# Two token groups at a time: a new tile order in the state-to-model projection, with its weight blocks loaded once per pair of groups

## The chip, the cores and the metric

The program runs on all 8 cores of one Trainium2 chip. Each core takes 4096 of the 32768 tokens and works alone on them; all weights are given to every core. The metric is the device time of the slowest core in microseconds (us). The engines of a core have names of their own in the profile: PE is TensorE, DVE is VectorE, ACT is ScalarE, POOL is GpSimd, SP is SyncE. PEq, ACTq and SPq are the sequencers that issue instructions and DMAs.

## The reference

The function is one layer of two residual blocks on x of 16 x 2048 x 2048, float32:

```python
x = x + (tanh(layernorm(x) @ B.T) @ C.T + D * layernorm(x))      # B: 1024 x 2048, C: 2048 x 1024
h = layernorm(x)
x = x + (silu(h @ Wg.T) * (h @ Wu.T)) @ Wd.T                     # hidden size 5632
```

Wg, Wu and Wd are bytes with zero point 128 and one scale for each output row. Layernorm has no gain or bias, eps 1e-5.

## The kernel before

A preparation stage turns the bytes of the weights into bfloat16 images in device memory. Then come 8 passes; pass p takes 512 tokens as four groups g = 0 to 3 of 128 tokens. A pass has these stages, in TensorE's program order:

- State: 16 chains of 16 matmuls 128x256 (line 504) make B times the normalised tokens, kept feature-major in HFM1. ScalarE takes the tanh into SFM (line 328).
- AT, the projection back to 2048 features, which the change touches: 16 tiles (g, s), where s = 0 to 3 is a block of 512 output features. A tile is 4 small matmuls with the diagonal of D (line 517) and 8 matmuls 128x512 (line 526) with the two halves of a C block as moving operand. C blocks lie in four buffers WCB0 to WCB3 of 512 KB: s = 0 and 2 use WCB0 and WCB1, s = 1 and 3 use WCB2 and WCB3. VectorE adds each finished tile to the token buffer XT (line 453, here called the evacuation) and counts it in EV_AT. A tile's PSUM bank is one of four, so TensorE waits at tile m for the evacuation of tile m-4.
- Second normalisation, group by group, in an order written out by hand on two engines: ScalarE squares the group (line 334), VectorE makes mean and variance, ScalarE the root (line 337), VectorE applies it into HTM0 or HTM1 (line 428), ScalarE's queue issues a transposing DMA into HFM2 (line 342).
- Gate and up: the first gate work is cut in halves of tokens. Two chains of 16 matmuls 128x256 over groups 0 and 1 wait for the transposes of groups 0 and 1; two more over groups 2 and 3 wait for the transposes of groups 2 and 3 (line 536). Then come full chains of 128x512 (lines 536 and 546) for 44 hidden blocks, and the down projection (line 602).

Here the AT stage's tiles run s-pair first: tiles 0 to 7 are (g 0..3) x (s 0, 1), tiles 8 to 15 are (g 0..3) x (s 2, 3). So every C block is loaded once per pass. The second pair of blocks (line 208 on SP's queue) waits for the semaphore MM_AT, TensorE's count of finished tiles, at 7 for WCB0 and WCB1 and at 8 for WCB2 and WCB3. The first pair of the next pass is loaded ahead, during the gate stage's end. Group 0 is complete after tile 9, group 1 after tile 11, groups 2 and 3 after tiles 13 and 15 (tiles counted from 0), and VectorE runs a group's normalisation at those points of its order.

Of the kernel before, what the change touches and what calls it, by code (L numbers as in the profile page):

```python
# [20 lines left out]
G = 4  # L21
# [26 lines left out]
def build_nc(n_pass):  # L48
# [21 lines left out]
    with ExitStack() as ctx:  # L70
# [38 lines left out]
        sem = {}  # L109
# [23 lines left out]
        for _p in range(n_pass):  # L133
            for _s in range(SL):
                for _j in range(11):
# [3 lines left out]
                    _cnt_wd[key] = _cnt_wd.get(key, 0) + 16  # L139
                    wd_info[_u] = (special, _u % 3, _cnt_wd[key])  # L140

        AT_TILES = [(g, 2 * sp + si) for sp in range(2) for g in range(G)
                    for si in range(2)]
        AT_BANK = [2 * (s % 2) + (g % 2) for (g, s) in AT_TILES]

        ST_ORDER = []
# [16 lines left out]
        @block.sync  # L163
        def _(sync):
            for apsrc, sb in [(sgc, SGC), (suc, SUC),
                              (dcol, DCOL), (ident, IDENT)]:
                sync.dma_start(out=sb[:], in_=apsrc).then_inc(sem["LDC"], 16)

            def emit_prep_load(u):
                kind, i = unit_kind(u)  # L170
                if kind == "D" and i % 11 == 0:
                    s_ = i // 11
                    if s_ > 0:
                        sync.wait_ge(sem["P_DQ"], NU_B + NU_C + NU_G + NU_U + 11 * s_)
                    sync.dma_start(out=SDP[:], in_=sdq[s_]).then_inc(sem["LSDP"], 16)
                if kind in ("B", "C"):
                    if u >= 2:
                        sync.wait_ge(sem["P_DQ"], u - 1)
                    w = D if kind == "B" else NCH * 512
                    src = bmi[i] if kind == "B" else cmi[i]  # L180
                    sync.dma_start(out=BF32[u % 2][:, :w], in_=src).then_inc(PLD1[u % 2], 16)
                else:
                    o = u - (NU_B + NU_C)
                    if o >= 10:
                        sync.wait_ge(sem["P_DQ"], u - 10 + 1)
                    src = wgi[i] if kind == "G" else (wui[i] if kind == "U" else wdi[i])
                    sync.dma_start(out=LQ[o % 10][:], in_=src).then_inc(PLD2[o % 10], 16)

            for u in range(NUNITS):
                emit_prep_load(u)  # L190

            for i in range(8):
                sync.wait_ge(PWR[i], PWR_FINAL[i])

            def emit_b(p, half, n):
                u = 16 * p + 8 * half + n
                if u >= 3:
                    sync.wait_ge(sem["MM_ST"], u - 2)
                sync.dma_start(out=WBB[u % 3][:], in_=sb_img[n]).then_inc(LWB[u % 3], 16)

            def emit_c(p, sp, si, h2_):
                s = 2 * sp + si
                slot = 2 * si + h2_
                if p > 0 or sp > 0:
                    pm = (16 * p + 8 * (sp - 1) + 7 + si) if sp > 0 \
                        else (16 * (p - 1) + 15 + si)
                    sync.wait_ge(sem["MM_AT"], pm)
                sync.dma_start(out=WCB[slot][:],
                               in_=sc_img[s][:, h2_ * 4:(h2_ + 1) * 4, :]
                               ).then_inc(LWC[slot], 16)  # L210

            def emit_gu(p, hc, is_up):
                t = 2 * (HC * p + hc) + is_up
                if t >= 3:
                    hc3 = (t - 3) // 2
                    if (t - 3) % 2 == 0:
                        sync.wait_ge(sem["MM_G"], hc3 + 1)
                    else:
                        sync.wait_ge(sem["MM_U"], hc3 + 1)
                sync.dma_start(out=WGU[t % 3][:],  # L220
                               in_=(su_img if is_up else sg_img)[hc]
                               ).then_inc(LWGU[t % 3], 16)

            for p in range(n_pass):
                for half in range(2):
                    for n in range(NCH):
                        if p > 0 and half == 0 and n < 3:
                            continue
                        emit_b(p, half, n)
                for sp in range(2):  # L230
                    for si in range(2):
                        for h2_ in range(2):
                            if p > 0 and sp == 0:
                                continue
                            emit_c(p, sp, si, h2_)
                for hc in range(HC):
                    for is_up in range(2):
                        if p > 0 and 2 * hc + is_up < 3:
                            continue
                        emit_gu(p, hc, is_up)  # L240
                if p + 1 < n_pass:
                    for n in range(3):
                        emit_b(p + 1, 0, n)
                    for si in range(2):
                        for h2_ in range(2):
                            emit_c(p + 1, 0, si, h2_)
                for s in range(SL):
                    for j in range(11):
                        u = HC * p + 11 * s + j
                        if wd_info[u][0]:  # L250
                            continue
                        if u >= 3:
                            sync.wait_ge(sem["FR_D"], u - 2)
                        sync.dma_start(out=WDB[u % 3][:],
                                       in_=sd_img[s * 11 + j]).then_inc(LWD[u % 3], 16)
                if p + 1 < n_pass:
                    for q in range(3):
                        emit_gu(p + 1, q // 2, q % 2)
            for b in range(NXB):
                n_st = len([1 for gi in range(4 * n_pass) if gi % NXB == b])  # L260
                if n_st:
                    sync.wait_ge(STX[b], 16 * n_st)
# [32 lines left out]
        def _(scalar):  # L295
# [27 lines left out]
            for p in range(n_pass):  # L323
# [5 lines left out]
                                      AF.Tanh).then_inc(sem["TANH"], 1)  # L329
                for g in range(G):  # L330
                    k = 8 * p + 4 + g
                    scalar.wait_ge(sem["EV_AT"], 16 * p + 2 * g + 10)
                    scalar.wait_ge(TPS[(k - 2) % 4], 16 * ((k - 2) // 4 + 1))
                    scalar.activation(HTM[k % 2][:], XT[xb(p, g)][:], AF.Square,  # L334
                                      accum_out=S2T[:, 4 + g:5 + g]).then_inc(sem["SQ_A"], 1)
                    scalar.wait_ge(sem["FIN"], k + 1)
                    scalar.activation(STDT[:, 4 + g:5 + g], VART[:, 4 + g:5 + g],
                                      AF.Sqrt).then_inc(sem["SQRT_A"], 1)
                    scalar.wait_ge(sem["APPLY"], k + 1)
                    if p > 0:  # L340
                        scalar.wait_ge(sem["MM_U"], HC * p)
                    scalar.dma_start(out=HFM2[:, :, g * 128:(g + 1) * 128],
                                     in_=HTM[k % 2][:], transpose=True).then_inc(TPS[k % 4], 16)
# [23 lines left out]
        def _(vector):  # L367
# [81 lines left out]
            for p in range(n_pass):  # L449
                def at_evac(m):  # L450
                    g, s = AT_TILES[m]
                    vector.wait_ge(sem["MM_AT"], 16 * p + m + 1)
# [2 lines left out]
                        1.0, XT[xb(p, g)][:, s * 512:(s + 1) * 512], ALU.mult, ALU.add,  # L455
                        accum_out=S1PT[:, g, s:s + 1]).then_inc(sem["EV_AT"], 1)

                for m in range(8):
                    at_evac(m)
                for g in range(G):  # L460
                    at_evac(8 + 2 * g)
                    at_evac(8 + 2 * g + 1)
                    k = 8 * p + 4 + g
                    vector.wait_ge(sem["EV_AT"], 16 * p + 2 * g + 10)
                    htm_free(k)
                    ds_inc(vector.tensor_scalar(TR4[:], S1PT[:, g, :], 1.0, 0.0, ALU.mult,
                                                ALU.add, accum_out=S1T[:, 4 + g:5 + g]))
                    ln_finalize(k, 4 + g, sqa=4 * p + g + 1)
                    ln_apply(k, 4 + g, xb(p, g))
# [19 lines left out]
        def _(tensor):  # L489
            tensor.wait_ge(sem["DDIAG_OK"], 1)  # L490
            for p in range(n_pass):
# [16 lines left out]
                for m in range(16):  # L508
                    g, s = AT_TILES[m]
# [5 lines left out]
                    for sub in range(4):  # L515
# [3 lines left out]
                                      DDIAG[:, dcg, :],  # L519
                                      start=(sub == 0), stop=False)  # L520
                    ins = None
                    for n in range(NCH):
                        if n % 4 == 0:
                            tensor.wait_ge(LWC[2 * (s % 2) + n // 4],
                                           16 * (2 * p + s // 2 + 1))
                        ins = tensor.matmul(PS[:, bank, :],  # L526
                                            SFM[:, n, g * 128:(g + 1) * 128],
                                            WCB[2 * (s % 2) + n // 4][:, n % 4, :],
                                            start=False, stop=(n == NCH - 1))
# [126 lines left out]
```

## Time and profile before

| | us |
|---|---|
| median of 3 runs | 5090.84 (5089.77 to 5103.79) |
| profiled execution | 5099.44 |
| its span, slowest core | 5097.9 |
| spans of the 8 cores | 5066.3 to 5097.9 |
| TensorE matmul busy | 4257.4 (84%) |
| granted TensorE clock, mean | 0.963 to 0.968 |

The span goes from the first instruction to the last on the slowest core, core 2, whose trace is read here. The profiled execution is 8.6 us above the median of the runs, and the time outside the span is 1.5 us. The preparation takes until about 465 us; after that one pass takes about 580 us. The eight AT stages begin at 510.5, 1085.3, 1667.3, 2256.7, 2834.5, 3416.5, 3991.8 and 4571.9 us.

### The profile page before, as it was taken

The numbers are of one execution on the slowest core, as the hardware profiler recorded it, in microseconds if no ns is written. First come the engines' busy times: TensorE is split into PE (matmuls) and PEld (weight loads), VectorE is DVE, ScalarE is ACT, GpSimd is POOL, SyncE is SP. The second block draws the span as 40 slices with busy tenths as digits, with TensorE's granted clock in tenths as the row PEclk, the third lists the DMA queues.
The fourth block names the chain that finished last, engine by engine and source line by source line (L and its number), as shares of the span: only waits on it lengthen the run. The fifth ranks groups of instructions, "written<-read, shape, count | busy, mean of one in ns | idle before, by whom it ended". The sixth has DMA issues, their size and how long they took to land.

```text
span 5097.9 us, 52159 instructions; the slowest of 8 cores (5066.3 to 5097.9 us)
## 1 busy us (share of the span) xinstructions
PE 4257.4 (84%) x20736; PEld 2048.7 (40%) x20736; DVE 936.7 (18%) x1408; ACT 397.7 (8%) x576; POOL 94.4 (2%) x179
## 2 busy tenths in 40 slices
PE   0002899979998899978999799988999799988998
PEld 0002444444444444444444444444444444444444
DVE  3465212021121111111120111211120211211100
ACT  0000100010100111001000101001100110001100
POOL 1210000000000000000000000000000000000000
PEclk9999999989999999989999899999999899999999
DMA  9987445554456445554455544554454544554544
GB/s 310 323 298 240 157 153 177 157 168 163 153 178 198 133 153 169 161 157 157 153 178 177 153 152 150 182 182 149 153 178 167 161 152 152 181 180 130 153 149 161
DMA packets 364905, 891.67 MB, mean 175 GB/s; under 512 B 159360, under 2 KB 159360, under 8 KB 353920
## 3 DMA queue, kind: packets, MB, share of 16 engines
q1 hardware_dynamic: 197136, 693.81, 41.7%
q10 hardware_dynamic: 142336, 100.68, 7.6%
q0 software_dynamic: 25200, 93.86, 5.5%
q8 instruction: 173, 2.83, 0.2%
q14 instruction: 60, 0.49, 0.0%
HBM read 743.53 MB, written 111.15 MB: 168 GB/s over the span
## 4 chain that ended last, share of the span: by engine, by line
PE 74%; DMA 17%; DVE 4%; ACT 2%; issue 1%; SPq 1%; ACTq 1%; DVEq 0%; POOLq 0%
PE PS L602 24%; PE PS L536 23%; PE PS L546 23%; PE PS L526 3%; DMA LQ<-wgi 2%; PE PS L504 2%; DMA WDB<-sd_img 2%; DMA LQ<-wui 2%; DMA WBB<-sb_img 2%; DMA HFM<-HTM 2%; DMA LQ<-wdi 1%; ACT HTM L334 1%; DMA XT<-xin 1%; DMA WCB<-sc_img 1%; DMA out<-XT 1%
## 5 line engine op out<-in xcount | busy, mean ns | idle before, releaser
L536 PE MATMUL PS<-HFM,WGU 128*128 128x512 bf16 (+1 forms) x5888 | 1308.1, 378 | 118.2 <-DMA HFM<-HTM 116.4
L546 PE MATMUL PS<-HFM,WGU 128*128 128x512 bf16 x5632 | 1280.5, 381 | 21.9 <-DMA WGU<-su_img 21.9
L602 PE MATMUL PS<-WDB,GFM 128*128 128x512 bf16 x5632 | 1233.5, 382 | 44.8 <-DMA WDB<-sd_img 44.8
L536 PEld LDWEIGHTS PS<-HFM,WGU 128*128 128x128 bf16 x5888 | 591.5, 101 | 781.9 <-issue 124.8
L602 PEld LDWEIGHTS PS<-WDB,GFM 128*128 128x128 bf16 x5632 | 554.9, 99 | 723.2 <-issue 69.8
L546 PEld LDWEIGHTS PS<-HFM,WGU 128*128 128x128 bf16 x5632 | 552.5, 98 | 692.1 <-issue 35.4
L504 PE MATMUL PS<-HFM,WBB 128*128 128x256 bf16 x2048 | 278.2, 303 | 609.2 <-DMA HFM<-HTM 526.7
L473 DVE SCALAR_TENSOR_TENSOR GFM<-PS,SUC,GFM 128x512 bf16<-128x512 f32 x352 | 264.6, 752 | 2233.3 <-PE PS L546 2233.3
L504 PEld LDWEIGHTS PS<-HFM,WBB 128*128 128x128 bf16 x2048 | 218.3, 108 | 669.1 <-issue 622.0
L351 ACT ACTIVATE GFM<-PS,SGC 128x512 bf16<-128x512 f32 x352 | 241.7, 687 | 2152.8 <-PE PS L536 2152.7
L526 PE MATMUL PS<-WCB,SFM 128*128 128x512 bf16 x1024 | 256.1, 394 | 24.6 <-DMA WCB<-sc_img 24.5
L481 DVE TENSOR_TENSOR XT<-XT,PS 128x512 f32<-128x512 f32 x128 | 79.4, 683 | 1045.9 <-PE PS L602 1045.9
L453 DVE SCALAR_TENSOR_TENSOR XT<-PS,XT 128x512 f32<-128x512 f32 x128 | 86.5, 689 | 400.7 <-PE PS L526 400.7
L526 PEld LDWEIGHTS PS<-WCB,SFM 128*128 128x128 bf16 x1024 | 96.7, 100 | 126.0 <-issue 42.6
L380 DVE TENSOR_SCALAR WOUT<-LQ 128x2048 bf16<-128x2048 uint8 x88 | 107.9, 1229 | 110.2 <-DMA LQ<-wui 56.6
L386 DVE SCALAR_TENSOR_TENSOR WOUT<-LQ,SDP 128x2048 bf16<-128x2048 uint8 x44 | 97.4, 2286 | 33.7 <-DMA LQ<-wdi 33.7
L312 ACT ACTIVATE STDT<-VART 128x1 f32<-128x1 f32 x32 | 6.5, 203 | 1243.4 <-DVE VART L416 1243.3
L291 POOL DMA_DIRECT2D WDB<-sd_img x31 | 16.7, 538 | 4599.8 <-PE PS L602 4599.8
L437 DVE TENSOR_SCALAR_CACHE_REDUCE HTM<-XT 128x2048 bf16<-128x2048 f32 x32 | 73.0, 2280 | 102.5 <-DMA XT<-xin 102.5
L428 DVE TENSOR_SCALAR HTM<-XT,MEANT,RSTDT 128x2048 bf16<-128x2048 f32 x64 | 86.2, 1346 | 6.9
L334 ACT ACTIVATE HTM<-XT 128x2048 bf16<-128x2048 f32 x32 | 61.1, 1910 | 296.1 <-DVE XT L453 292.0
L441 DVE SCALAR_TENSOR_TENSOR HTM<-XT 128x2048 bf16<-128x2048 f32 x32 | 73.4, 2293 | 3.4
(29 smaller groups left out, 349.6 us busy)
## 6 DMA issues: line engine op xcount, KB each, us to landing
WGU<-sg_img SPq DMA_DIRECT2D x352, 512.0 KB, 3.5
WGU<-su_img SPq DMA_DIRECT2D x352, 512.0 KB, 3.5
WDB<-sd_img SPq DMA_DIRECT2D x321, 512.0 KB, 3.5
WBB<-sb_img SPq DMA_DIRECT2D x128, 512.0 KB, 5.7
XT<-xin ACTq DMA_DIRECT2D x32, 1024.0 KB, 8.3
WCB<-sc_img SPq DMA_DIRECT2D x64, 512.0 KB, 6.9
out<-XT ACTq DMA_DIRECT2D x32, 1024.0 KB, 8.8
sg_img<-WOUT POOLq DMA_DIRECT2D x44, 512.0 KB, 14.2
```

Of the source, the lines that this page charges most:

```text
L334: scalar.activation(HTM[k % 2][:], XT[xb(p, g)][:], AF.Square, accum_out=S2T[:, 4 + g:5 + g]).then_inc(sem["SQ_A"], 1)
L351: scalar.activation(GFM[:, hc, :], PS[:, 4 + hc % 2, :], AF.Silu, scale=SGC[:, hc:hc + 1]).then_inc(sem["SILU"], 1)
L380: vector.tensor_scalar_add(WOUT[u % 8][:, :D], LQ[o % 10][:], -128.0).then_inc(sem["P_DQ"], 1)
L386: vector.scalar_tensor_tensor(WOUT[u % 8][:, :D], LQ[o % 10][:], -128.0, SDP[:], ALU.add, ALU.mult).then_inc(sem["P_DQ"], 1)
L428: vector.tensor_scalar(HTM[k % 2][:], XT[b][:], MEANT[:, i:i + 1], RSTDT[:, i:i + 1], ALU.subtract, ALU.mult).then_inc(sem["APPLY"], 1)
L453: vector.scalar_tensor_tensor(XT[xb(p, g)][:, s * 512:(s + 1) * 512], PS[:, AT_BANK[m], :], 1.0, XT[xb(p, g)][:, s * 512:(s + 1) * 512], A ...
L473: vector.scalar_tensor_tensor(GFM[:, hc, :], PS[:, 6 + hc % 2, :], SUC[:, hc:hc + 1], GFM[:, hc, :], ALU.mult, ALU.mult).then_inc(sem["GMU ...
L504: ins = tensor.matmul(PS[:, n, lo:hi], WBB[u % 3][:, c, :], HFM1[:, c, lo:hi], start=(c == 0), stop=(c == DC - 1))
L526: ins = tensor.matmul(PS[:, bank, :], SFM[:, n, g * 128:(g + 1) * 128], WCB[2 * (s % 2) + n // 4][:, n % 4, :], start=False, stop=(n == NC ...
L536: ins = tensor.matmul(PS[:, 4 + hc % 2, lo:hi], WGU[t % 3][:, c, :], HFM2[:, c, lo:hi], start=(c == 0), stop=(c == DC - 1))
L546: ins = tensor.matmul(PS[:, 6 + hc % 2, lo:hi], WGU[t % 3][:, c, :], HFM2[:, c, lo:hi], start=(c == 0), stop=(c == DC - 1))
L602: ins = tensor.matmul(PS[:, bank, :], GFM[:, hc, g * 128:(g + 1) * 128], WDB[u % 3][:, q * 512:(q + 1) * 512], start=(hc == 0), stop=(hc = ...
```

## The change

The 16 tiles run in another order: group pair first. Tiles 0 to 3 are (g 0, 1) x (s 0, 1), tiles 4 to 7 are (g 0, 1) x (s 2, 3), tiles 8 to 11 are (g 2, 3) x (s 0, 1), tiles 12 to 15 are (g 2, 3) x (s 2, 3). Groups 0, 1, 2 and 3 are complete after tiles 5, 7, 13 and 15. The C blocks are loaded in four blocks `blk` of four DMAs per pass in place of two, and the waits and counts follow.

```diff
-        AT_TILES = [(g, 2 * sp + si) for sp in range(2) for g in range(G)
-                    for si in range(2)]
+        AT_TILES = [(2 * gp + gi, 2 * sp + si) for gp in range(2) for sp in range(2)
+                    for gi in range(2) for si in range(2)]
...
-            def emit_c(p, sp, si, h2_):
-                s = 2 * sp + si
+            def emit_c(p, blk, si, h2_):
+                s = 2 * (blk % 2) + si
                 slot = 2 * si + h2_
-                if p > 0 or sp > 0:
-                    pm = (16 * p + 8 * (sp - 1) + 7 + si) if sp > 0 \
+                if p > 0 or blk > 0:
+                    pm = (16 * p + 4 * blk - 1 + si) if blk > 0 \
                         else (16 * (p - 1) + 15 + si)
                     sync.wait_ge(sem["MM_AT"], pm)
...
-                for sp in range(2):
+                for blk in range(4):
                     for si in range(2):
                         for h2_ in range(2):
-                            if p > 0 and sp == 0:
+                            if p > 0 and blk == 0:
                                 continue
-                            emit_c(p, sp, si, h2_)
+                            emit_c(p, blk, si, h2_)
...
-                    scalar.wait_ge(sem["EV_AT"], 16 * p + 2 * g + 10)
+                    scalar.wait_ge(sem["EV_AT"], 16 * p + (6, 8, 14, 16)[g])
...
-                for m in range(8):
-                    at_evac(m)
+                AT_LAST = (5, 7, 13, 15)
+                _m = 0
                 for g in range(G):
-                    at_evac(8 + 2 * g)
-                    at_evac(8 + 2 * g + 1)
+                    while _m <= AT_LAST[g]:
+                        at_evac(_m)
+                        _m += 1
                     k = 8 * p + 4 + g
-                    vector.wait_ge(sem["EV_AT"], 16 * p + 2 * g + 10)
+                    vector.wait_ge(sem["EV_AT"], 16 * p + AT_LAST[g] + 1)
...
+                    blk = 2 * (g // 2) + s // 2
                     for n in range(NCH):
                         if n % 4 == 0:
                             tensor.wait_ge(LWC[2 * (s % 2) + n // 4],
-                                           16 * (2 * p + s // 2 + 1))
+                                           16 * (4 * p + blk + 1))
```

On VectorE, at the AT stage of pass 0 (XT0 to XT3 are the four groups' token buffers; rows of line 453 evacuate a tile, the row of line 466 or 467 begins a group's normalisation):

```order
 L453 SCALAR_TENSOR_TENSOR XT0,S1PT<-PS,XT0 128x512 x2
 L453 SCALAR_TENSOR_TENSOR XT1,S1PT<-PS,XT1 128x512 x2
-L453 SCALAR_TENSOR_TENSOR XT2,S1PT<-PS,XT2 128x512 x2
-L453 SCALAR_TENSOR_TENSOR XT3,S1PT<-PS,XT3 128x512 x2
-L453 SCALAR_TENSOR_TENSOR XT0,S1PT<-PS,XT0 128x512 x2
-L466 TENSOR_SCALAR TR4,S1T<-S1PT 128x4
+L453 SCALAR_TENSOR_TENSOR XT0,S1PT<-PS,XT0 128x512 x2
+L467 TENSOR_SCALAR TR4,S1T<-S1PT 128x4
```

Group 0's normalisation stands after 6 evacuations in place of 10.

On VectorE, further on in the same stage, between the normalisations of group 1 and group 2:

```order
 L428 TENSOR_SCALAR HTM1<-XT1,MEANT,RSTDT 128x2048
 L453 SCALAR_TENSOR_TENSOR XT2,S1PT<-PS,XT2 128x512 x2
-L466 TENSOR_SCALAR TR4,S1T<-S1PT 128x4
+L453 SCALAR_TENSOR_TENSOR XT3,S1PT<-PS,XT3 128x512 x2
+L453 SCALAR_TENSOR_TENSOR XT2,S1PT<-PS,XT2 128x512 x2
+L467 TENSOR_SCALAR TR4,S1T<-S1PT 128x4
```

Six evacuations stand between these two normalisations in place of two; groups 2 and 3 keep their places, after 14 and 16 evacuations.

On SP's queue, at the end of the C block loads of pass 0:

```order
 L208 DMA WCB2<-sc_img 128x2048 [waits MM_AT]
 L208 DMA WCB3<-sc_img 128x2048 [waits MM_AT]
+L208 DMA WCB0<-sc_img 128x2048 [waits MM_AT]
+L208 DMA WCB1<-sc_img 128x2048 [waits MM_AT]
+L208 DMA WCB2<-sc_img 128x2048 [waits MM_AT]
+L208 DMA WCB3<-sc_img 128x2048 [waits MM_AT]
```

The same four rows follow once more: 8 DMAs of 512 KB are added in every pass, ahead of the gate stage's loads. ScalarE's order is the same as before. TensorE's has the same shapes in a row, with other groups and C blocks behind them.

## Rows read from the trace of the kernel before

**Rows 1.** The page: busy time by engine, and the WCB load's issues.
```profile
PE 4257.4 (84%) x20736; PEld 2048.7 (40%) x20736; DVE 936.7 (18%) x1408; ACT 397.7 (8%) x576; POOL 94.4 (2%) x179
...
WCB<-sc_img SPq DMA_DIRECT2D x64, 512.0 KB, 6.9
```

**Rows 2.** Waits of TensorE (who <- for whom: us in total, times, longest us).
```profile
PE PS L536 <- DMA HFM<-HTM: 116.4, 16, 8.2
...
PE PS L526 <- DMA WCB<-sc_img: 24.5, 18, 3.3
```

**Rows 3.** Timeline of pass 1, TensorE: start, duration, what, [idle before <-releaser].
```profile
1085.25 0.38 PE L517 MATMUL PS<-DDIAG,HFM 128*128 128x128 bf16 x4 [0.95 <-ACT SFM L328]
...
1104.02 1.02 PE L526 MATMUL PS<-WCB,SFM 128*128 128x512 bf16 x4 [2.79 <-DMA WCB<-sc_img]
...
1105.27 1.87 PE L526 MATMUL PS<-WCB,SFM 128*128 128x512 bf16 x4 [0.22 <-DMA WCB<-sc_img]
...
1107.35 2.41 PE L526 MATMUL PS<-WCB,SFM 128*128 128x512 bf16 x8
...
1119.85 1.89 PE L526 MATMUL PS<-WCB,SFM 128*128 128x512 bf16 x8
...
1128.73 5.37 PE L536 MATMUL PS<-HFM,WGU 128*128 128x256 bf16 x32 [6.99 <-DMA HFM<-HTM]
...
1142.07 5.53 PE L536 MATMUL PS<-HFM,WGU 128*128 128x256 bf16 x32 [7.97 <-DMA HFM<-HTM]
```

**Rows 4.** The same timeline of pass 1: VectorE, ScalarE and the two DMA queues.
```profile
1087.47 0.69 DVE L453 SCALAR_TENSOR_TENSOR XT<-PS,XT 128x512 f32<-128x512 f32 x1 [31.05 <-PE PS L526]
...
1099.14 2.75 SPq L208 DMA_DIRECT2D WCB<-sc_img  x4
...
1099.17 0.69 DVE L453 SCALAR_TENSOR_TENSOR XT<-PS,XT 128x512 f32<-128x512 f32 x1 [1.25 <-PE PS L526]
...
1109.87 0.69 DVE L453 SCALAR_TENSOR_TENSOR XT<-PS,XT 128x512 f32<-128x512 f32 x1 [1.93 <-PE PS L526]
...
1110.71 1.91 ACT L334 ACTIVATE HTM<-XT 128x2048 bf16<-128x2048 f32 x1 [25.72 <-DVE XT L453]
...
1117.06 1.85 ACTq L342 DMA_TRANSPOSE HFM<-HTM  x1
...
1124.13 1.78 ACTq L342 DMA_TRANSPOSE HFM<-HTM  x1
...
1126.06 1.91 ACT L334 ACTIVATE HTM<-XT 128x2048 bf16<-128x2048 f32 x1 [3.78 <-DVE XT L453]
...
1137.68 1.92 ACTq L342 DMA_TRANSPOSE HFM<-HTM  x1
```

**Rows 5.** Timelines of passes 2 and 4: first matmul, and tile 9's evacuation.
```profile
1667.25 0.38 PE L517 MATMUL PS<-DDIAG,HFM 128*128 128x128 bf16 x4 [0.95 <-ACT SFM L328]
...
1691.18 0.69 DVE L453 SCALAR_TENSOR_TENSOR XT<-PS,XT 128x512 f32<-128x512 f32 x1 [1.58 <-PE PS L526]
...
2834.54 0.38 PE L517 MATMUL PS<-DDIAG,HFM 128*128 128x128 bf16 x4 [0.95 <-ACT SFM L328]
...
2860.30 0.69 DVE L453 SCALAR_TENSOR_TENSOR XT<-PS,XT 128x512 f32<-128x512 f32 x1 [2.51 <-PE PS L526]
```

**Rows 6.** Stretches of pass 1: busy us of each engine, PEclk, DMA share, GB/s.
```profile
1116.90:1121.90 5.00, 4.72 (x28) 2.04 (x25) 1.86 (x10) 2.00 (x2) 0.00 (x0) 1.00 0.56 105
...
1099.10:1108.80 9.70, 6.69 (x33) 2.98 (x31) 2.10 (x6) 0.00 (x0) 0.00 (x0) 0.82 0.67 216
1099.10:1104.00 4.90, 2.14 (x16) 1.03 (x14) 1.40 (x4) 0.00 (x0) 0.00 (x0) 1.00 0.74 186
1104.00:1108.80 4.80, 4.56 (x17) 1.95 (x18) 0.70 (x2) 0.00 (x0) 0.00 (x0) 0.64 0.61 247
```

**Rows 7.** Line 317, the first normalisation's transposes, which run beside WBB loads.
```profile
L317 ACTq DMA_TRANSPOSE HFM<-HTM x32: 1334/2151/4104, 452.9 to 4542.7; - x32
...
DMA to landing us min/median/max: 4.3/6.1/15.6
```

## The prediction

> **What bounds the kernel now.** I read the page first: TensorE's matmuls are busy for 84% of the span and no other engine comes near it [rows 1], so time is won or lost only where TensorE stands still. TensorE's list of waits comes next, and two of its rows belong to the edited stage [rows 2]: the gate stage's wait for the transposes into HFM2, 116.4 us in 16 waits, so two of 7.3 us in each of the 8 passes, and the AT stage's wait for C blocks, 24.5 us in all, so 3.1 us a pass. The change trades one for the other. To price the trade I follow one pass, pass 1, in the timeline, on TensorE [rows 3] and on the engines around it [rows 4]. All times below count from the first matmul of its AT stage, 1085.25.
>
> The first evacuation starts at 2.22 (1087.47). The seventh starts at 1099.17, 11.70 later for 6 tiles: a tile takes 1.95 us. Then the C blocks are exchanged. Call this a refill. Its four loads are issued from 1099.14 on, when tile 6 is done, so only tile 7 covers them: WCB0 is there at 1104.02 and WCB1 at 1105.27, 4.9 and 6.1 us after the issue. The evacuation of tile 9 starts at 1109.87, which is 24.62. Without the refill it would be 2.22 + 9 x 1.95 = 19.77, so a refill costs 4.85 us, more than the 2.79 + 0.22 us of idle time beside it. The rest is the clock: the granted clock is 1.00 in the 4.9 us from the issue and 0.64 in the next 4.8 [rows 6], after TensorE stood idle for 2.79; four matmuls take 1.87 us there and the next eight 2.41 [rows 3]. In passes 2 and 4 tile 9's evacuation starts at 23.93 and 25.76 [rows 5], so the refill costs 4.16 and 5.99. The mean of the three is 5.0.
>
> From tile 9 on, nothing of TensorE sets the end. Squaring of group 0 starts 0.84 after the evacuation (1110.71), and the four groups follow each other through ScalarE, VectorE and the issue of the transpose, until the last transpose is issued at 1137.68 and the second half of the gate work starts at 1142.07, which is 56.82. TensorE has been ready since 1119.85 + 1.89 and fills the time with only one piece of 5.37 us, at 1128.73.
>
> **The change part by part.** *What it removes.* Groups 0 and 1 complete before tile 8, so their normalisation lies beside tiles 6 to 12, and their 13.4 us of chain (transposes issued 1117.06 and 1124.13, the second 13.4 after the first squaring) leave the path. What is late next is group 2, complete only after tile 13, and group 3 behind it. Their part can be read off: squaring of group 2 at 1126.06 to the gate work at 1142.07 is 16.01 us. With the 0.84 before it, 16.85 us from the evacuation of tile 13. The half chains over groups 0 and 1 start at once after tile 15 and are over long before; they cost nothing. Group 3's tiles 14 and 15 are done 2 x 1.95 us after tile 13, inside group 2's chain, as it is today.
>
> *What it adds.* Each pass has three refills in place of one, because each C block is used by two groups before its buffer is taken for another. The loads of each refill are again issued one tile before they are needed (MM_AT 3, 7, 11 for WCB0 and WCB1, needed by tiles 4, 8, 12). 64 more loads of 512 KB in all. Behind the waiting loads on SP's queue stand only the gate stage's loads, and in passes 1 to 7 the first three of those are already there, so nobody else waits.
>
> The sum, with refill 1 at pass 1's own 4.85 and the two new ones at 5.0: tile 13's evacuation starts at 2.22 + 13 x 1.95 + 4.85 + 10.0 = 42.42, the gate work's second half at 42.42 + 16.85 = 59.27, against 56.82. That is 2.45 us a pass later, 19.6 us in 8 passes. The break-even is a new refill at 3.8 us. With both at 4.16 the sum is +0.8 a pass (+6 us), with both at 5.99 it is +4.4 (+35 us).
>
> *A collision that the trace of before does not have.* Refills 2 and 3 now meet transposes. A transpose takes 0.56 x 5.0 = 2.8 us of all the DMA engines, a refill 0.67 x 9.7 = 6.5 us, of which 0.74 x 4.9 = 3.6 lie in the first 4.9 us after the issue [rows 6]; so it works from 1.3 to 7.8 us after its issue. Group 0's squaring starts 0.84 after tile 5's evacuation (2.22 + 9.75 + 4.85 = 16.8), its transpose is issued 7.2 us after that evacuation as today (1109.87 to 1117.06), at 24.0, and works until 28. Refill 2 is issued with tile 6 done, at 18.8, and works from 20.1 to 26.6: an overlap of some 1.3 us. Group 1's transpose is issued 7.1 later, at 31.1, and works from 32.4 to 35.2; refill 3, issued at 31.6, works from 32.9 to 39.4: an overlap of 2.3, and its first block is the one that TensorE stands waiting for. The lower end is 0, if the loads go first or the clock's share of the refill hides the delay; a gain is excluded, as more traffic brings no load sooner. The near upper end is the whole of both overlaps, 3.6 us a pass. The nearest rows on mixed traffic are the transposes of the first normalisation, which run beside WBB loads and stores: 6.1 us to landing in the median, 15.6 at most, 4.3 at best [rows 7]. I take half of 3.6, that is 1.8 a pass or 14 us, since the rows show each kind filling the engines and none going first.
>
> The Trainium skill ("DMA: Bandwidth & Descriptors", section "Issuing engines are not separate DMA queues") says that DMAs of ScalarE's and SP's queues end up on the same 16 DMA engines and interleave. By that rule a load and a transpose both lose; without it the sum would stop at +20. No run here shows a C load beside a transpose yet.
>
> *Edits that cost nothing.* TensorE's wait for the evacuation of tile m-4: VectorE is in group 0's normalisation from 16.8 to 24.0 and in group 1's until 31.1, with evacuations 6 and 7 between. Tile 12 needs evacuation 8, done by 32, and its C block does not come before 36. Were this cover gone, each microsecond of refill 3 saved would be lost here again from about 4 us on. ScalarE's order is unchanged.
>
> **Sum.** 19.6 + 14 = 34 us. The profiled execution is 5099.44, with 1.5 us outside its span, and would become about 5134; it lies 8.6 above the median of the runs, 5090.84, and I put the difference on that median: 5125.
>
> **The rivals.**
>
> A, the forecast: new refills near 5 us, partly stretched. 5110 to 5146 (+20 to +35 by the refills' spread, 0 to 29 for the overlaps, not both at their ends). 0.50.
>
> B, no collision, new refills at 5.0: +20, 5111. For it: two thirds of each refill lie outside the transposes. Against it: refill 3 does not. 0.14.
>
> C, heavy collision: the small packets of the transposes hold the loads back for more than their own work. Landings of 15.6 us [rows 7] speak for it; against it, those also lie beside 1 MB stores. If the overlapped 3.6 us are stretched as the slowest of those transposes is, 15.6 / 4.3 = 3.6 times, they become 13, which is 9.4 us later a pass, 75 in 8, on top of 20: 5186. From 5147 on I count it here. 0.16.
>
> D, the new refills are all as cheap as the cheapest seen, 4.16, and the transposes hide: +6, 5097. 0.13.
>
> E, the other side: a new refill costs only its first idle gap. If TensorE's clock stays at 2.4 GHz, its higher level, through the new refills, because each is followed and preceded by dense tiles, and the second and third buffers arrive under running tiles, each costs 2.8 us in place of 5.0. Then the gate work starts at 2.22 + 25.35 + 4.85 + 5.6 + 16.85 = 54.87, 1.95 sooner than now: -16 us, 5075. It decides from below 3.8 us a refill. Against it: all three refills read above cost over 4.1, and the clock fell to 0.64 after one idle gap of 2.8. 0.07.
>
> **How the numbers follow.** A measurement of this kernel tells about 0.3%, or 15 us, from no change: slower is above 5106, faster below 5076. A, B and C are slower: 0.80. D and a part of E are within: 0.15. The rest of E is faster: 0.05. The time is A's, 5125. The range 5097 to 5160 holds A, B, a part of D and the near part of C; the likeliest case alone is 5110 to 5146.
>
> **What would show it.** Waits of TensorE: the C block row near 24.5 x 3, with some 50 waits, where C loads before had 18; the transposes' row falls from 116.4 to about 76 (one wait a pass, 16.85 less 3.9 for tiles 14 and 15 and 3.5 for the first half chains at full clock, 9.5), since the first half chains wait for nothing. Timeline of a pass: tile 13's evacuation 42 to 45 after the AT stage's start, the second half of the gate work at 59 to 63, and the half chains over groups 0 and 1 directly behind tile 15. Granted clock below 1 after each of the three refills. A median landing of C loads above 6.9 [rows 1]. I am wrong if tile 13's evacuation starts before 40, or if the distance from it to the gate work is not about 17, or if TensorE waits for VectorE at tile 12.

## The result and the profile after

The changed kernel is slower: the ratio to the kernel before is 1.0121, with a 95% interval of 1.0097 to 1.0145, so 49 to 74 us. (Many of the runs, of both kernels, had one die at a lower granted clock; they set the medians over all runs, 5189.23 and 5170.76 us, while the ratios here leave them out, and "not determined" stands where too few others are left.) The profiled execution took 5153.61 us, its slowest core 5152.1, against 5099.44 and 5097.9 before. The forecast was +34 us, with slower at 0.80. On the median of before, 5090.84, the ratio makes 5152 us: above the likeliest case (5110 to 5146) and in the stretch that the prediction gave to rival C (from 5147 on).

The page after, for [rows 1]:

```profile
PE 4264.8 (83%) x20736; PEld 2046.6 (40%) x20736; DVE 935.4 (18%) x1408; ACT 397.6 (8%) x576; POOL 96.9 (2%) x179
...
WCB<-sc_img SPq DMA_DIRECT2D x128, 512.0 KB, 6.8
```

TensorE's waits after, for [rows 2] (us in total, times, longest):

```profile
PE PS L528 <- DMA WCB<-sc_img: 127.4, 61, 15.9
...
PE PS L538 <- DMA HFM<-HTM: 72.6, 8, 9.8
...
PE PS L548 <- DMA WGU<-su_img: 13.6, 7, 2.8
PE PS L518 <- DVE XT L453: 2.5, 3, 1.0
```

The transposes' waits fall from 116.4 to 72.6 us, one a pass, as forecast (76). The waits for C blocks rise from 24.5 to 127.4 where 73 was forecast (24.5 x 3), in 61 waits where 50 were, and the longest is 15.9 us. Pass 1 of the changed kernel shows where, for [rows 3] and [rows 4]; times in the text count from its AT start, 1109.50:

```profile
1109.50 0.38 PE L518 MATMUL PS<-DDIAG,HFM 128*128 128x128 bf16 x4 [0.95 <-ACT SFM L328]
...
1122.74 0.69 DVE L453 SCALAR_TENSOR_TENSOR XT<-PS,XT 128x512 f32<-128x512 f32 x1 [4.47 <-PE PS L528]
...
1131.83 1.02 PE L528 MATMUL PS<-WCB,SFM 128*128 128x512 bf16 x4 [2.04 <-DMA WCB<-sc_img]
...
1132.96 4.20 ACTq L342 DMA_TRANSPOSE HFM<-HTM  x1
...
1142.73 5.82 ACTq L342 DMA_TRANSPOSE HFM<-HTM  x1
...
1148.94 1.02 PE L528 MATMUL PS<-WCB,SFM 128*128 128x512 bf16 x4 [0.17 <-DMA WCB<-sc_img]
...
1156.82 1.87 PE L528 MATMUL PS<-WCB,SFM 128*128 128x512 bf16 x4 [6.85 <-DMA WCB<-sc_img]
...
1158.80 0.69 DVE L453 SCALAR_TENSOR_TENSOR XT<-PS,XT 128x512 f32<-128x512 f32 x1 [9.55 <-PE PS L528]
1158.91 3.52 PE L528 MATMUL PS<-WCB,SFM 128*128 128x512 bf16 x8
...
1164.21 3.66 PE L538 MATMUL PS<-HFM,WGU 128*128 128x256 bf16 x32
...
1171.26 1.93 ACTq L342 DMA_TRANSPOSE HFM<-HTM  x1
...
1175.65 0.59 PE L538 MATMUL PS<-HFM,WGU 128*128 128x256 bf16 x2 [7.78 <-DMA HFM<-HTM]
```

Refills 1 and 2 go as forecast: tile 5 is evacuated from 16.3 (1125.77; 16.8 forecast) and refill 2 holds TensorE for 2.04 us at tile 8. Refill 3 does not. Its last block arrives at 1156.82, in the middle of tile 13, after 6.85 us of waiting. Tile 13's evacuation starts at 49.3 (1158.80), where the sum had 42.4 to 46. From there to the second half of the gate work it is 16.85 us, exactly as forecast. The half chains over groups 0 and 1 (1164.21) follow tile 15 directly and take 3.66 us in place of 5.37.

ScalarE's queue shows the other party. Issuing group 0's transpose takes 4.20 us where it took 1.85 [rows 4], so group 1 follows late: its transpose is issued at 33.2, not 31.1. Refill 3's first two loads were issued at 31.0, when tile 10 was done, and its second two at 33.0 to 33.4, so the transpose leaves with the second two. Issuing it takes 5.82 us. Landing of the second normalisation's 32 transposes (line 342):

```profile
DMA to landing us min/median/max: 4.2/4.9/22.1
```

Landing of the 128 C loads (line 208):

```profile
DMA to landing us min/median/max: 4.0/6.8/21.6
```

One transpose took 22.1 and one C load 21.6 us, while the medians, 4.9 and 6.8, hardly moved (4.3 and 6.9 before): the damage sits in a few transfers. Over all cores and passes it is group 1's transpose that lands late, 13.8 us after its issue on average (4.3 before); groups 2 and 3 land after 4.3 as before, group 0 after 6.0. The stretches of refill 3 in pass 1, with the columns of [rows 6]:

```profile
1142.70:1156.80 14.10, 5.18 (x20) 1.89 (x21) 3.04 (x10) 0.00 (x0) 0.00 (x0) 0.71 1.11 166
...
1145.00:1148.00 3.00, 2.81 (x8) 0.84 (x7) 0.04 (x2) 0.00 (x0) 0.00 (x0) 0.52 1.19 238
...
1154.00:1157.00 3.00, 0.18 (x1) 0.14 (x2) 0.00 (x0) 0.00 (x0) 0.00 (x0) 0.50 1.07 72
```

All DMA engines stay busy (a share above 1 means that packets' times overlap in the records), but what they move falls from 238 to 72 GB/s. Their busy time in this stretch, the time of all packets over 16 engines, is 1.11 x 14.1 = 15.7 us. I call it engine time; where the share is above 1 it can hold waiting as well as work. A refill alone was 6.5 and a transpose alone 2.8 [rows 6].

**The same over all cores.** From every core's timeline I took the time from the first matmul of the AT stage to the start of the second half of the gate work, here "the stretch". Each value is the mean of 8 cores x 8 passes. The ratio is to the kernel before.

| kernel | stretch, us | AT stage alone, us | ratio (95%) |
|---|---|---|---|
| before | 57.16 | 36.56 | 1 |
| changed | 65.03 | 52.60 | 1.0121 (1.0097 to 1.0145) |
| hold_transposes | 58.90 | 45.40 | 1.0058 (1.0036 to 1.0081) |
| hold_group1_only | 59.67 | 46.13 | not determined |
| plain_copy | 60.15 | 46.58 | 1.0062 (1.0036 to 1.0087) |
| timed_plain | 61.91 | 48.38 | 1.0101 (1.0077 to 1.0126) |
| kept_old_order | 52.49 | 31.88 | 0.9832 (0.9809 to 0.9854) |
| kept_new_order | 49.80 | 36.63 | 0.9798 (0.9763 to 0.9832) |
| kept_late_group1 | 45.24 | 31.91 | 0.9712 (0.9692 to 0.9732) |
| kept_group_major | 42.91 | 32.18 | 0.9682 (0.9648 to 0.9716) |
| kept_group_major_fill | other stage | 32.04 | 0.9689 (0.9665 to 0.9713) |
| group_major_fill_late_x | other stage | 32.21 | 0.9581 (0.9532 to 0.9629) |

The last six kernels of the table keep C blocks on chip. In the last two the first gate work is cut at another token, so the stretch would end at another piece of work ("other stage"). The change costs 7.87 us a pass in the stretch, 63 us in 8. From the stretch's end to the next AT stage the mean goes from 522.41 to 520.70, 12 us back in 7 passes. Together 51 us; the profiled spans differ by 54, the ratio says 61.

### The profile page after: what moved, and what is told of

Same layout as the page of the kernel before. It is cut to its first block, busy times and chain, and to the rows that moved or that the text cites. A ratio compares the mean times of both kernels' runs of the same rounds, so it can differ in the third digit from the quotient of the medians.

```text
span 5152.1 us, 52287 instructions; the slowest of 8 cores (5121.6 to 5152.1 us)
## 1 busy us (share of the span) xinstructions
PE 4264.8 (83%) x20736; PEld 2046.6 (40%) x20736; DVE 935.4 (18%) x1408; ACT 397.6 (8%) x576; POOL 96.9 (2%) x179
## 4 chain that ended last, share of the span: by engine, by line
PE 74%; DMA 19%; DVE 3%; issue 1%; SPq 1%; ACT 1%; ACTq 0%; DVEq 0%; POOLq 0%
PE PS L604 23%; PE PS L538 23%; PE PS L548 22%; DMA WCB<-sc_img 4%; PE PS L528 3%; PE PS L505 2%; DMA WDB<-sd_img 2%; DMA WBB<-sb_img 2%; DMA HFM<-HTM 2%; DMA su_img<-WOUT 1%; DMA sg_img<-WOUT 1%; DMA XT<-xin 1%; DMA out<-XT 1%; DMA LQ<-wdi 1%; DMA LQ<-wgi 1%
## 5 line engine op out<-in xcount | busy, mean ns | idle before, releaser
L538 PE MATMUL PS<-HFM,WGU 128*128 128x512 bf16 (+1 forms) x5888 | 1289.9, 374 | 73.1 <-DMA HFM<-HTM 72.6
L528 PE MATMUL PS<-WCB,SFM 128*128 128x512 bf16 x1024 | 287.8, 425 | 127.6 <-DMA WCB<-sc_img 127.4
```

The costliest lines, as they stand in the source:

```text
L528: ins = tensor.matmul(PS[:, bank, :], SFM[:, n, g * 128:(g + 1) * 128], WCB[2 * (s % 2) + n // 4][:, n % 4, :], start=False, stop=(n == NC ...
L538: ins = tensor.matmul(PS[:, 4 + hc % 2, lo:hi], WGU[t % 3][:, c, :], HFM2[:, c, lo:hi], start=(c == 0), stop=(c == DC - 1))
```

## The experiments

My theory after the result: refill 3 and group 1's transpose meet on the DMA engines, and together they take more engine time than one after the other. The rival: refills are simply dearer than 5 us when there are three of them, through device memory or the clock.

**Hold both transposes.** Before the transposes of groups 0 and 1 ScalarE waits for the refill in flight:

```diff
+                    if g in (0, 1):
+                        for i in range(4):
+                            scalar.wait_ge(LWC[i], 16 * (4 * p + 3 + g))
                     scalar.dma_start(out=HFM2[...], in_=HTM[k % 2][:], transpose=True)
```

> The changed kernel, but ScalarE's queue issues the transposes of groups 0 and 1 only when the refill in flight (refill 2, refill 3) has landed. From AT start to the second half of the gate work, mean over 8 cores and 8 passes: 57.16 us before, 65.03 changed. Theory 'collision': the transposes hold refill 3 back; with them out of the way the stretch is 59.2 to 60, as the sum without a collision had it, the time falls by 5 to 6 us a pass, about 43 us, ratio to before about 1.004, and the waits for C blocks fall from 127 us to about 75. Rival 'refills are dearer by themselves' (device memory or clock): no change, 65 us and ratio 1.012.

The stretch was 58.90 us: 6.1 of the 7.87 us are gone, by nothing but a later issue, with the three refills still there. The rival is out as the cause of these 6.1 us. TensorE's waits on core 0, this profile's slowest:

```profile
PE PS L541 <- DMA HFM<-HTM: 78.8, 11, 10.1
...
PE PS L531 <- DMA WCB<-sc_img: 56.7, 53, 4.7
...
PE PS L521 <- DVE XT L456: 20.9, 8, 3.9
```

The C blocks' row fell below the forecast (about 75), to 56.7, but VectorE's rose to 20.9: the held transpose of group 0 pushes group 1's normalisation back, and tile 12 waits for evacuation 8, beside the refill it would wait for anyway. In pass 1 of core 2 refill 3 and the transpose stand apart:

```profile
1116.30:1124.70 8.40, 3.38 (x15) 1.48 (x14) 4.48 (x13) 2.21 (x3) 0.00 (x0) 0.83 0.85 298
1124.70:1129.70 5.00, 4.78 (x19) 2.14 (x19) 0.70 (x2) 0.00 (x0) 0.00 (x0) 0.60 0.56 105
```

That is 0.85 x 8.4 = 7.1 and 0.56 x 5.0 = 2.8 us of engine time, 9.9 in all, against 15.7 when they met. (The first stretch also holds the end of group 0's held transpose.) Counted over all cores and passes 1 to 7, from the first issue of refill 3 and group 1's transpose to the last landing of the two, for 2.6 MB each time, it is 14.1 us in the changed kernel and 9.4 with group 1's transpose held (the next run).

**Hold group 1's only** (`if g in (1,)`).

> The changed kernel with only group 1's transpose held until refill 3 has landed; group 0's is issued beside refill 2 as in the changed kernel. Holding both gave 58.90 us from the AT start to the second half of the gate work, the changed kernel 65.03. If all of the loss lies in refill 3 and group 1's transpose: 59 to 60, ratio as with both held, about 1.006. Rival, group 0's transpose costs its share too (it may still be in flight when refill 3 starts): 61 to 62.5, ratio about 1.009.

59.67 us. Group 1's transpose in refill 3 makes 5.4 of the 6.1 us, group 0's the other 0.8. The first reading holds. TensorE's wait for C blocks is 70.4 us here, close to the 73 forecast for three refills without a collision, and its wait for VectorE only 4.0.

**A plain copy in place of the transposes**, in passes 1 to 7:

```diff
+                    if p > 0 and g < 2:
+                        scalar.dma_start(out=GFM[:, 8 + 4 * g:12 + 4 * g, :],
+                                         in_=HTM[k % 2][:]).then_inc(TPS[k % 4], 16)
+                        continue
```

> The changed kernel; in passes 1 to 7 the transposing DMAs of groups 0 and 1 are replaced by plain DMAs of the same 512 KB, between the same engines and at the same place, into an unused part of GFM (so HFM2 keeps the groups 0 and 1 of pass 0; the output is not the reference's). If it is the kind of the transfer, its 2080 small packets, that holds refill 3 back: near 60 us for the stretch, ratio about 1.004. If any 512 KB beside a refill would do it: between 61 and 65, ratio 1.007 to 1.012. If refills are dearer by themselves: 65 and 1.012.

60.15 us, which looks like "the kind of transfer". But the moment changed too: a plain copy is issued in 0.5 us, so group 1's left on average 0.7 us ahead of refill 3's first load, where the changed kernel's transpose leaves 1.6 us behind it. This run cannot tell kind from timing.

**The same moment, two kinds.** Group 0's copy is plain in both, and group 1's transfer waits for tile 10, so it leaves with refill 3, once as a plain copy and once as a transpose:

```diff
+                    if p > 0 and g == 1:
+                        scalar.wait_ge(sem["MM_AT"], 16 * p + 11)
```

> The changed kernel; in passes 1 to 7 group 0's transpose is a plain DMA of 512 KB into an unused part of GFM, and so is group 1's, which is issued only when tile 10 is done (MM_AT 11), in the moment in which refill 3 is issued (the output is not the reference's). With plain_copy group 1's copy left before refill 3, so that it could not tell kind from timing. If the kind of transfer makes the loss: the stretch stays near 60 us, at most 61.5, and the engines' work in refill 3 is about 6.5 + 1.7 us. If any transfer of 512 KB in this moment does it: 63 or more.

> The same kernel with one difference: group 1's transfer is the transposing DMA again, issued in the same moment (MM_AT 11); group 0's stays a plain copy (the output is not the reference's). Theory 'kind': 64 to 66 us as in the changed kernel, 4 to 5 more than timed_plain, and the engines' work in refill 3 above 12 us. Rival 'two transposes in a row are needed' (group 0's still in flight): 61 or less. Rival 'any transfer': the same as timed_plain.

Over passes 1 to 7 the stretch is 61.70 us (standard error 0.27) with the plain copy and 65.05 (0.44) with the transpose; but cores 4 to 7 had a granted clock of 0.90 in the transpose's profile. On cores 0 to 3 alone, with 0.963 to 0.966 and 0.958 to 0.963, it is 61.65 and 64.23. The transpose's ratio is not determined. Over the same passes the copies that left early give 59.75, holding group 1's transpose 59.28, and holding both 58.55. The truth lies between my two theories: 512 KB of any kind in this moment cost 2 to 3 us a pass (61.70 less 59.75, 59.28 or 58.55), and that it is a transpose another 2.6. The stretches after the issue on core 2, pass 1, with the plain copy:

```profile
1114.40:1119.40 5.00, 2.05 (x13) 0.92 (x11) 2.33 (x8) 0.00 (x0) 0.00 (x0) 1.00 0.91 256
1119.40:1124.40 5.00, 4.47 (x18) 1.70 (x17) 0.70 (x2) 0.00 (x0) 0.00 (x0) 0.66 0.66 269
1124.40:1127.40 3.00, 3.00 (x22) 1.59 (x21) 0.86 (x4) 1.73 (x1) 0.00 (x0) 1.00 0.00 0
```

And with the transpose:

```profile
1116.60:1121.60 5.00, 2.06 (x14) 0.92 (x11) 2.30 (x8) 0.00 (x0) 0.00 (x0) 1.00 0.94 226
1121.60:1126.60 5.00, 2.62 (x10) 0.94 (x8) 0.70 (x2) 0.00 (x0) 0.00 (x0) 0.57 1.08 194
1126.60:1131.60 5.00, 4.06 (x13) 1.73 (x14) 0.38 (x1) 0.00 (x0) 0.00 (x0) 0.50 0.59 104
```

7.9 us of engine time with the plain copy, 13.1 with the transpose, for the same bytes; over all cores and passes 1 to 7, counted as above, 7.9 and 13.0. The rival that needs two transposes in a row is out: here group 0's is a plain copy.

**No refills.** The tanh output moves into an unused part of GFM, six C half blocks stay on chip for the whole kernel, and only the two of s = 3 are loaded once a pass:

```diff
-        SFM = E(nc.sbuf_tensor("SFM", [128, NCH, T], BF16))
+        SFM = GFM
-        WCB = [... for i in range(4)]
+        WCB = [... for i in range(6)]
...
+                dst = WCB[2 * s + h2_][:] if s < 3 else \
+                    GFM[:, 24 + 4 * h2_:28 + 4 * h2_, :]
```

> The tile order of before with the same kept C blocks and no refill: it prices the refill of before alone. My price of 4.9 us a refill gives 52.3 for the stretch, -39 us, ratio 0.992. If only the idle gap counts (3.3 us): -26 us, 0.995. The difference to the new order with kept blocks is what the new order is worth by itself: about 63 us.

> The changed kernel's tile order without refills: SFM lies in a part of GFM, six C half blocks (s = 0 to 2) stay on chip for the whole kernel, and the two of s = 3 are loaded once a pass into an unused part of GFM around the AT stage's start. Both theories: no refill left, tile 13's evacuation at 27.6 and the second half of the gate work at 44.4 after the AT start, 12.7 a pass earlier than before, 102 us in all, ratio about 0.980. If the normalisation chain of groups 0 and 1 on VectorE then stops TensorE (tile 12 waits for evacuation 8), some 2 to 4 us a pass less of it, ratio 0.983 to 0.986.

With the old order the stretch was 52.49 us, as priced (52.3), so a refill is worth 4.7 us and not only its idle gap. The ratio 0.9832 is 85 us, twice the forecast. The other half has another place:

```profile
PE PS L530 <- DMA HFM<-HTM: 117.4, 16, 8.4
...
PE PS L596 <- DMA WDB<-sd_img: 3.2, 2, 2.8
```

The down stage's wait for its first D blocks fell from 44.8 us before to 3.2. Before, four C loads for the next pass stood ahead of these D loads on SP's queue; now they are gone. I had counted the removed loads at nothing. That they are what held the D loads back is likely but not shown, as no run took out these four alone; the same row fell from 42.0 us in the changed kernel to 5.6 with the new order and kept blocks.

With the new order the stretch was 49.80, not 44.4. The second reading of the expectation came true, and larger:

```profile
PE PS L511 <- DVE XT L446: 26.0, 9, 3.5
```

On core 2, pass 1, the last matmuls of tile 11 and the first of tile 12:

```profile
1086.35 1.89 PE L521 MATMUL PS<-WCB,GFM 128*128 128x512 bf16 x8
1091.62 0.38 PE L511 MATMUL PS<-DDIAG,HFM 128*128 128x128 bf16 x4 [3.37 <-DVE XT L446]
```

VectorE is in group 1's normalisation when tile 12 needs evacuation 8: 3.37 us of standing, and a granted clock of 0.66 in the 5 us behind it. So the new tile order as written is worth 2.7 us a pass even with no refill at all. It needs one more edit:

```diff
-                AT_LAST = (5, 7, 13, 15)
+                AT_LAST = (5, 9, 13, 15)
```

> The new tile order with kept C blocks, and VectorE takes evacuations 8 and 9 ahead of group 1's normalisation (AT_LAST of group 1 is 9). Kept blocks alone gave 49.80 us where the sum without stalls has 44.4, and TensorE waited for VectorE at tile 12 (3.37 us in pass 1, then half clock). If that wait is the whole missing part: 44.5 to 46 us, 4 to 5 us a pass, ratio about 0.973. Rival, the chain of groups 2 and 3 itself is longer than read: 49 us stays, 0.980.

45.24 us and 0.9712: the wait was 4.6 of the 5.4 us that were missing, and VectorE's row is back to 0.4 us.

**A version that beats both.** With all C blocks on chip the tiles can go group by group, banks `m % 4`:

```diff
+        AT_TILES = [(g, s) for g in range(G) for s in range(SL)]
+        AT_BANK = [m % 4 for m in range(16)]
```

> Kept C blocks and tiles group by group, (g, s) with s inside, banks m % 4; each group is complete 4 tiles after the one before. VectorE's cycle for a group (7.2 us of chain and 4 evacuations, about 7.7) then just fits TensorE's 4 tiles (7.8). Sum: squarings at 8.9, 18, 25.8 and 33.6, second half of the gate work at 43.1 after the AT start against 49.8: 6.7 a pass, 54 us, ratio about 0.969. If each group's chain stops TensorE as in the new order (3 us a group and half clock): 50 or more, ratio 0.98 or above.

42.91 us (43.1 forecast), ratio 0.9682. What is left is one wait of some 7 us for group 3's transpose. The next edit fills it by cutting the first gate and up chains at token 384:

```diff
-                    gate_chain(hc, 0, 256, False)
+                    gate_chain(hc, 0, 384, False)
+                up_chain(0, 0, 384, False)
...
-                    gate_chain(hc, 256, 512, True)
+                    gate_chain(hc, 384, 512, True)
+                up_chain(0, 384, 512, True)
```

> The same, and the first gate and up work is cut at token 384 in place of 256: three chains over groups 0 to 2 (gate 0, gate 1, up 0) fill the wait for group 3's transpose, then three of 128 tokens over group 3. Sum: the three long chains take 7.7 us from 35.3 on, the short ones 3 us from 43.1, where now 3.4 to 5.5 of half chains and 3.4 of up 0 follow: 4 to 6 us a pass less, 32 to 48 us, ratio about 0.961. If the short chains of 128 columns are dearer than their columns, nothing is gained: 0.969.

The time stayed (0.9689), and not for the reason that the second reading gives. The chains came where they should, but nothing was won, because the next wait took the gain:

```profile
1103.67 5.36 PE L531 MATMUL PS<-HFM,WGU 128*128 128x384 bf16 x32 [3.62 <-DMA HFM<-HTM]
...
1113.25 1.06 PE L541 MATMUL PS<-HFM,WGU 128*128 128x128 bf16 x16
1123.31 4.52 PE L541 MATMUL PS<-HFM,WGU 128*128 128x512 bf16 x15 [9.00 <-DMA WGU<-su_img]
```

Up 1 waits 9.00 us for its weights, which are loaded beside 3 MB of tokens; this row went from 10.7 us in all to 51.5. Moving those token loads behind gate blocks 8, 12 and 16:

```diff
+                    if hc in (8, 12, 16) and p + 1 < n_pass:
+                        emit_xload(p + 1, hc // 4 - 2)
```

> Kept C blocks, tiles group by group, and the three loads of the next pass's tokens are issued from ScalarE's queue ahead of gate blocks 8, 12 and 16 instead of directly behind the last transpose. The wait for WGU<-su_img at the stage's start is 10.7 us in 7 waits with group-major tiles; moved loads should take most of it: 8 us less, ratio 0.967 against 0.968. If those waits have nothing to do with the token loads: no change.

> The cut at token 384 with the token loads moved in the same way. With the cut alone the time stayed (0.9689 against 0.9682) and TensorE waited 51.5 us in 8 waits for WGU<-su_img, which is loaded beside 3 MB of tokens. If the token loads cause it: the load lands about 3.5 us after its issue, the wait shrinks from 9 to about 3 us, 5 to 6 us in 7 passes, 35 to 40 us, ratio about 0.961. If the wait is that WGU0 comes free too late, only 1 to 2 us a pass are won: 0.966.

The ratio of the first of the two is not determined; on its core 4 the row for WGU<-su_img has 0.3 us left of 10.7, but the row for the D blocks has 14.9 where it had 5.1, so whether time was won stays open. The second reached 0.9581 (0.9532 to 0.9629), 4879.79 us in its profiled execution. TensorE's waits there:

```profile
PE PS L530 <- DMA HFM<-HTM: 27.4, 8, 3.6
PE PS L540 <- DMA WGU<-su_img: 22.6, 12, 4.1
```

## Why the prediction was wrong

The direction and the trade were right, the size was not: +34 forecast, 49 to 74 measured. The step that failed is the price of the collision of refills 2 and 3 with the transposes: 1.8 us a pass forecast, 6.1 measured, of which 5.4 lie in refill 3 and group 1's transpose.

- *Two waits of 7.3 us become one.* Right: 72.6 us in 8 waits, 76 forecast.
- *A refill costs 5.0 us.* Right, within 0.3. Tile 5's evacuation at 16.3 against 16.8; the old order without its refill came out 4.7 us shorter; and with group 1's transpose held, three refills cost 59.67 less 45.24, so 4.8 each.
- *Tail of 16.85 us behind tile 13's evacuation.* Right to the hundredth in pass 1.
- *The sum without a collision, 59.27 us.* It matches the runs in which the transposes were held (58.90, 59.67). The match is partly luck with both held, since a wait for VectorE stood in for part of refill 3 there.
- *The collision, "half of 3.6, that is 1.8 a pass".* This is the step that failed. Measured it is 65.03 less 58.90, so 6.1 us a pass. Two things were wrong in it. First, and small, the time of meeting: I let group 1's transpose leave at 31.1, half a us ahead of refill 3, but the stretched issue of group 0's (4.20 us) delayed it to 33.2, two us behind refill 3's first load. By my own working times that raises the overlap only from 2.3 us to the transpose's whole 2.8. Second, and decisive, I took the engines' work as conserved: 6.5 + 2.8 = 9.3 us, in whatever order. It was 15.7 in pass 1, and 14.1 on average against 9.4 apart. My upper end, the whole of both overlaps, rested on the same assumption and was no bound. Rival C had the right mechanism ("hold the loads back for more than their own work"), and I gave it 0.16 and a price of 9.4 us; the truth lies between A and C. Not all of it is the small packets of a transpose: the plain copy in the same moment cost 2 to 3 us too.
- *TensorE does not wait for VectorE at tile 12.* Wrong as written, and I had named it a sign of being wrong: it waits there in 3 of core 2's passes (2.5 us in all), and in 37 of 64 over all cores, up to 1.3 us. It costs next to nothing, for the reason given: refill 3, which tile 12 needs anyway, comes later still. The runs with kept blocks took that cover away, and the same wait was worth 4.6 us of stretch (49.80 less 45.24).
- *The other signs.* The half chains came directly behind tile 15, as forecast. Tile 13's evacuation (49.3) and the second half of the gate work (66.2 in pass 1) came later than the 42 to 45 and 59 to 63 named. The median landing of C loads did not rise above 6.9 (it is 6.8), and in pass 1 the granted clock fell behind refills 1 and 3 (0.66 and 0.50 over 5 us) but not behind refill 2 (1.00).
- *The Trainium skill's rule* that DMAs of the two queues interleave on the same 16 engines ("DMA: Bandwidth & Descriptors", section "Issuing engines are not separate DMA queues") agrees with the held transposes: issuing one of ScalarE's transfers a pass later shortened TensorE's wait for SP's, from 127.4 us to 70.4. That the two together take more engine time than apart the rule does not say; the runs do.

What stays open: the ratios of the held and of the timed runs are larger than their stretches explain. With both transposes held the stretch is 1.7 us longer than before, 14 us in all, and the ratio says 29 (18 to 41); the timed plain copies have 38 by the stretch and 51 by the ratio. The held kernel's profiled execution, 5097.87 us, was its quickest (median of all 9 runs 5115.33), so its trace shows a quick sample. Of the engine time, no run tells why a transpose and loads together take more than apart.

## What to carry to other kernels

Before you move a transfer to an earlier place, list what else is on the DMA engines in that microsecond, and price a meeting above the sum of the two works; for a transpose that met a burst of loads it was 1.5 times the sum here (14.1 against 9.4 us). Weigh an order that finishes half of the work early against the operands that it has to load again: here the earlier finish was worth 7.3 us a pass (52.49 to 45.24), and two more refills cost 4.8 each. Keeping the blocks on chip, with one evacuation point moved, turned the same order from 1.2% slower to 2.9% faster; the old order with kept blocks was 1.7% faster. And after each wait that you remove, look for the one behind it: VectorE's normalisation at tile 12, then the weights of up 1.

## What the runs showed of the hardware

A transposing DMA is sensitive at both ends. On core 2 its issue on ScalarE's queue took 1.33 to 1.96 us before and up to 7.79 beside a refill, its landing 4.2 to 6.0 and up to 22.1, and the C loads took 21.6 in place of 11.5 at most. A plain copy of the same 512 KB was issued in 0.5 us. The issue time matters by itself, since ScalarE's next squaring stands behind it. And the engine time of a refill together with 512 KB more was 13.0 us with a transpose and 7.9 with a plain copy in the same moment, 9.4 with the transpose behind the refill.
